# A 64-channel mix on four 64x64 quarters of TensorE's array, with the row sum issued ahead of it

## Chip, cores and metric

The kernel runs on one core of a Trainium2 chip. The metric is the device time of one execution in microseconds, the median over runs. Engines are called PE (TensorE: matmuls, with its weight loads shown apart as PEld), DVE (VectorE), ACT (ScalarE), POOL (GpSimd) and SP (SyncE, which here issues every DMA).

## What is computed

```
x        [64, 64, 1024] f32     itok     [64] int, 0..15
weights  [16, 64, 64]   f32     qweight  [1024, 768] int32 (6-bit values, 3 words -> 4 values)
scale, zero [1024, 1]           bias     [1024]

y   = einsum('bct,bcd->bdt', x, weights[itok])       # the "mix": a 64x64 matrix per batch entry
w   = (unpack6(qweight) - zero) * scale              # [1024, 1024]
out = x + einsum('bsk,nk->bsn', y, w) + bias
```

## The kernel before

**Tiles.** Two batch entries make a tile of 128 rows (entry 2t in partitions 0 to 63, entry 2t+1 in 64 to 127), so there are TILES = 32 tiles. The two 64x64 mixing matrices of a tile stand as blocks on the diagonal of `w_sb[:, slot, :]` (128x128, the other two blocks are zero; the DMAs of `load_w` fill only the diagonal). x, the mixing matrices and the results y have rings of RING = 4 slots.

**Mix.** `mix(j, i)` (L231) makes y transposed: for each of KT = 8 chunks of 128 positions, x's chunk is the stationary operand (128 rows of channels by 128 columns of positions) and the block-diagonal matrix is the moving one (128 columns). The result, 128 positions by 128 (entry, channel) columns, goes to `y_ps[:, j % 2, kt, :]`, a buffer of two PSUM banks per tile, used in turn by even and odd tiles. Both operands are f32. The trace shows two weight loads and two matmuls for each such call in the program, 16 pairs a tile. The semaphore `y_ps_ready` rises after chunk 3 and again after chunk 7.

**Row sum.** `sum_y` (L246) multiplies the same mixing matrices with a column of row sums of x (`xsum`, made by ACT at L336) into `ysum_ps`. It takes the zero point of the quantized weights out of the product later on (`residual`, L426).

**Splitting y.** ACT's `high` (L339) copies each half of y_ps to `y_hi` in the rounded type fp32r as soon as its semaphore rises; DVE's `low` (L417) subtracts it and writes the rest to `y_lo`.

**Linear layer.** `linear(j, i, h)` (L266) makes one 512-column half h of the output: 16 matmuls of 512 columns (8 chunks, y_hi and y_lo), from the unpacked integer weights `qT` in SBUF, into `o_ps[:, h]`. DVE multiplies it by the scale (`scale_out`, L434), adds the residual (`add_residual`, L445), and SP stores it. POOL adds x and bias into `resid` (L527).

**Order.** It is written out by hand for every engine. In the steady part `step(j, i)` of PE (L282) does the mix of the tile LEAD = 3 ahead, its row sum, and then the two halves of the linear layer of tile j. `mix` waits for x, for the mixing matrices, and for `y_lo` of the tile two before (its PSUM buffer); `linear(…, 0)` waits for `y_lo` of its own tile, `linear(…, h)` for the scaled output half of the tile before. Ahead of the loop a written-out start interleaves the first mixes with the unpacking and transposing of the quantized weights (`unpack_q` on DVE, `transpose_q` on PE, `place_q` on ACT). The last half of the last tile uses a y_ps bank as one of two 256-column output pieces.

Of the kernel before, what the change touches and what calls it, by code (L numbers as in the profile page):

```python
# [18 lines left out]
F32 = mybir.dt.float32  # L19
# [12 lines left out]
def adaln_ffn(nc: bass.Bass, x, cond, weights, qweight, scale, zero, bias, out):  # L32
# [19 lines left out]
    with ExitStack() as ctx:  # L52
# [6 lines left out]
        def sem(name):  # L59
# [20 lines left out]
        resid = sb("resid", [P, RING, N], F32)  # L80
        o_sb = sb("o_sb", [P, 2, N], F32)

        y_ps = psum("y_ps", [P, 2, KT, P], F32)
        o_ps = psum("o_ps", [P, H, NH], F32)
        ysum_ps = psum("ysum_ps", [P, 512], F32)
        qt_ps = psum("qt_ps", [P, KT, P], BF16)
# [3 lines left out]


        last_pieces = [(o_ps[:, 1, 0:NH // 2], NH, NH // 2),
                       (y_ps[:, 0, 0:KT // 2, :].rearrange("p t r -> p (t r)")[:, 0:NH // 2], NH + NH // 2, NH // 2)]


        ids_loaded = sem("ids_loaded")
# [132 lines left out]

        @block.tensor  # L230
        def _(pe):  # L231
            def mix(j, i):

                t = i * RING + j
                slot = j % RING
                x_arrived(pe, j, i)
                pe.wait_ge(w_loaded[slot], (i + j // RING + 1) * 32)
                if not isinstance(t, int) or t >= 2:
                    pe.wait_ge(y_lo_ready, (t - 1) * 2)
                for kt in range(KT):  # L240
                    last = nc.tensor.matmul(y_ps[:, j % 2, kt, :], x_sb[:, slot, kt * P:(kt + 1) * P],  # L241
                                            w_sb[:, slot, :], start=True, stop=True)
                    if kt % (KT // 2) == KT // 2 - 1:
                        last.then_inc(y_ps_ready, 1)

            def sum_y(j, i):  # L246

                t = i * RING + j
                slot = j % RING
                pe.wait_ge(w_loaded[slot], (i + j // RING + 1) * 32)  # L250
                pe.wait_ge(xsum_ready, t + 1)
                if not isinstance(t, int) or t >= 1:
                    pe.wait_ge(ysum_ready, t)
                nc.tensor.matmul(ysum_ps[:, slot:slot + 1], w_sb[:, slot, :], xsum[:, slot:slot + 1],  # L254
                                 start=True, stop=True).then_inc(ysum_ps_ready, 1)

            def transpose_q(n):
                pe.wait_ge(q_cast, n + 1)
                if n >= 2:
                    pe.wait_ge(qt_ready, n - 1)  # L260
                for kt in range(KT):
                    last = nc.tensor.transpose(qt_banks[n % 2][:, kt, :], q_bf[:, n % 4, kt * P:(kt + 1) * P],  # L262
                                               ident[:])
                last.then_inc(qt_ps_ready, 1)

            def linear(j, i, h):  # L266
                t = i * RING + j
                if h == 0:
                    pe.wait_ge(y_lo_ready, t * 2 + 2)
                if not isinstance(t, int) or t >= 1:  # L270
                    pe.wait_ge(scaled[h], t)
                products(o_ps[:, h, :], h * NH, NH, j % RING).then_inc(o_ps_ready[h], 1)

            def products(bank, col, width, slot):
                for kt in range(KT):
                    for part in (y_hi, y_lo):
                        last = nc.tensor.matmul(bank, part[:, slot, kt, :], qT[:, kt, col:col + width],  # L277
                                                start=(kt == 0 and part is y_hi),
                                                stop=(kt == KT - 1 and part is y_lo))
                return last  # L280

            def step(j, i, mixes=True):  # L282
                if mixes:
                    mix(j + LEAD, i)
                    sum_y(j + LEAD, i)
                for h in range(H):
                    linear(j, i, h)


            pe.wait_ge(warm_ready, 1)  # L290
            for _ in range(WARMUP):
                nc.tensor.matmul(ysum_ps[:], warm[:, 0:P], warm[:], start=True, stop=True)  # L292
            mix(0, 0)
            sum_y(0, 0)
            pe.wait_ge(ident_ready, 1)
            for n in range(NT // 2):
                transpose_q(n)
            mix(1, 0)
            pe.wait_ge(qt_ready, NT // 2)
            linear(0, 0, 0)  # L300
            sum_y(1, 0)
            mix(2, 0)
            sum_y(2, 0)
            transpose_q(4)
            transpose_q(5)
            linear(1, 0, 0)
            transpose_q(6)
            transpose_q(7)
            linear(2, 0, 0)
            mix(3, 0)  # L310
            sum_y(3, 0)
            pe.wait_ge(qt_ready, NT)
            for j in range(3):
                linear(j, 0, 1)
                mix(j + RING, 0)
                sum_y(j + RING, 0)
            for h in range(H):
                linear(3, 0, h)
            with pe.Fori(1, TRIPS - 1) as i:
                for j in range(RING):  # L320
                    step(j, i)
            for j in range(RING - 1):
                step(j, TRIPS - 1, mixes=j + LEAD < RING)
            linear(RING - 1, TRIPS - 1, 0)
            pe.wait_ge(scaled[1], TILES - 1)
            for bank, col, width in last_pieces:
                products(bank, col, width, RING - 1).then_inc(o_ps_ready[1], 1)


        @block.scalar  # L330
        def _(act):
            def sum_x(j, i):
                x_arrived(act, j, i)
                if not isinstance(i, int) or i * RING + j >= RING:
                    act.wait_ge(ysum_ps_ready, i * RING + j - RING + 1)
                nc.scalar.activation(junk[:], x_sb[:, j % RING, :], ACT.Copy,  # L336
                                     accum_out=xsum[:, j % RING:j % RING + 1]).then_inc(xsum_ready, 1)

            def high(j, i):  # L339
                t = i * RING + j  # L340
                for half in range(2):

                    act.wait_ge(y_ps_ready, t * 2 + half + 1)
                    chunks = slice(half * KT // 2, (half + 1) * KT // 2)
                    nc.scalar.activation(y_hi[:, j % RING, chunks, :], y_ps[:, j % 2, chunks, :],  # L345
                                         ACT.Copy).then_inc(y_hi_ready, 1)

            def copy_ysum(j, i):
                t = i * RING + j
                act.wait_ge(ysum_ps_ready, t + 1)  # L350
                if not isinstance(t, int) or t >= RING:
                    act.wait_ge(resid_ready, t - RING + 1)
                slot = j % RING
                nc.scalar.activation(ysum[:, slot:slot + 1], ysum_ps[:, slot:slot + 1],
                                     ACT.Copy).then_inc(ysum_ready, 1)

            def place_q(n):
                act.wait_ge(qt_ps_ready, n + 1)
                nc.scalar.activation(qT[:, :, n * P:(n + 1) * P], qt_banks[n % 2], ACT.Copy).then_inc(qt_ready, 1)

            sum_x(0, 0)
            high(0, 0)
            copy_ysum(0, 0)
            for n in range(NT // 2):
                place_q(n)
            high(1, 0)
            sum_x(1, 0)
            copy_ysum(1, 0)
            sum_x(2, 0)
            high(2, 0)  # L370
            copy_ysum(2, 0)
            place_q(4)
            place_q(5)
            sum_x(3, 0)
            place_q(6)
            place_q(7)
            high(3, 0)
            copy_ysum(3, 0)
            sum_x(4, 0)

            def step(j, i, highs=True, sums=True):
                if highs:
                    high(j + LEAD, i)
                    copy_ysum(j + LEAD, i)
                if sums:
                    sum_x(j + LEAD + 1, i)

            for j in range(1, RING):
                step(j, 0)
            with act.Fori(1, TRIPS - 1) as i:  # L390
                for j in range(RING):
                    step(j, i)
            step(0, TRIPS - 1, sums=False)
# [3 lines left out]
        def _(dve):  # L397
# [19 lines left out]
            def low(j, i):  # L417
                t = i * RING + j
                for half in range(2):
                    dve.wait_ge(y_hi_ready, t * 2 + half + 1)  # L420
                    chunks = slice(half * KT // 2, (half + 1) * KT // 2)
                    nc.vector.tensor_tensor(y_lo[:, j % RING, chunks, :], y_ps[:, j % 2, chunks, :],  # L422
                                            y_hi[:, j % RING, chunks, :].bitcast(F32),
                                            ALU.subtract).then_inc(y_lo_ready, 1)

            def residual(j, i):  # L426
# [131 lines left out]
```

## Time and profile before

| | us |
|---|---|
| median of 3 runs | 325.77 (323.64 to 326.3) |
| the profiled execution, its own time | 325.39 |
| its span, first to last instruction | 323.3 |
| mean granted TensorE clock (share of full) | 0.989 |

In the profile, PE's matmul records overlap, because one begins before the one ahead of it has left the array. The distance from start to start is what a matmul costs in a stream; the duration is how long it takes from its start to its last result. Weight loads (PEld) are records of their own beside the matmuls.

### The profile page before, as it was taken

To read this page: it belongs to the slowest core of one execution; us is meant where nothing else is said; L and a number is where in the kernel's file an instruction comes from. 1 tells how busy PE (TensorE), PEld (TensorE's weight loads), DVE (VectorE), ACT (ScalarE), POOL (GpSimd) and SP (SyncE) were. 2 spreads that over 40 slices of the span, in tenths; PEclk is the share of its full clock that TensorE was granted. 3 is DMA by queue.
4 is the path that set the end of the run, shared out by engine and by line. 5 is a ranking of instruction groups with operands and counts; after the bars stand their busy time and mean duration, and the time that the engine had idled before them with its cause. 6 is when DMAs were issued, how large, how long until landed. Compare 5 with 4: busy or idle time off the path is not lost.

```text
span 323.3 us, 5312 instructions
## 1 busy us (share of the span) xinstructions
PE 310.3 (96%) x1700; PEld 264.8 (82%) x1700; DVE 211.4 (65%) x261; ACT 82.6 (26%) x169; POOL 78.2 (24%) x39
## 2 busy tenths in 40 slices
PE   8892899999999999999999999999999999999995
PEld 3782788888888888888888888888888888888885
DVE  3589983776666667666666676666667766666553
ACT  3762153222221122222212222221122222210000
POOL 1009123222221222222112222221122222212000
PEclk9998699999999999999999999999999999999999
DMA  6992165532332333323333332233332311101122
GB/s 208 317 336 70 51 212 176 169 133 89 120 134 101 134 123 110 114 88 132 123 112 134 101 130 101 102 134 107 129 134 101 130 69 65 65 32 67 65 83 80
DMA packets 20684, 39.46 MB, mean 122 GB/s; under 512 B 6850, under 2 KB 7106, under 8 KB 20674
## 3 DMA queue, kind: packets, MB, share of 16 engines
q1 hardware_dynamic: 20674, 39.33, 35.1%
q8 instruction: 5, 0.08, 0.1%
q14 instruction: 5, 0.04, 0.0%
HBM read 22.54 MB, written 16.78 MB: 122 GB/s over the span
## 4 chain that ended last, share of the span: by engine, by line
PE 90%; DVE 5%; SPq 1%; DMA 1%; issue 1%; DVEq 0%
PE o_ps L277 72%; PE y_ps L241 17%; DMA q_raw<-in_L_ffn_qweight_dram 1%; DVE q_int L405 1%; DVE q_int L407 1%; DVE q_int L409 1%; PE ysum_ps L254 1%; DVE q_bf L414 1%; PE y_ps L277 1%; PE o_ps L262 1%; DVE y_lo L422 0%; SPq L145 0%; SPq L141 0%; SPq L136 0%; SPq L174 0%
## 5 line engine op out<-in xcount | busy, mean ns | idle before, releaser
L277 PE MATMUL o_ps<-qT,y_hi 128*128 128x512 f32 (+1 forms) x512 | 201.8, 395 | 0.0
L277 PE MATMUL o_ps<-qT,y_lo 128*128 128x512 f32 (+1 forms) x512 | 199.1, 390 | 0.0
L527 POOL TENSOR_TENSOR resid<-x_sb,bias_bc 128x1024 f32<-128x1024 f32 x32 | 77.0, 2411 | 213.8 <-DVE o_sb L450 192.2
L277 PEld LDWEIGHTS o_ps<-qT,y_lo 128*128 128x128 f32 x512 | 96.8, 189 | 19.1
L277 PEld LDWEIGHTS o_ps<-qT,y_hi 128*128 128x128 f32 x512 | 96.8, 189 | 18.9
L442 DVE TENSOR_TENSOR o_sb<-o_ps,scale_bc 128x512 f32<-128x512 f32 x63 | 43.6, 692 | 87.8 <-PE o_ps L277 87.8
L345 ACT ACTIVATE y_hi<-y_ps 128x512 fp32r<-128x512 f32 x64 | 38.3, 599 | 194.3 <-PE y_ps L241 194.3
L241 PEld LDWEIGHTS y_ps<-w_sb,x_sb 128*128 128x128 f32 x512 | 61.9, 191 | 2.4
L241 PE MATMUL y_ps<-w_sb,x_sb 128*128 128x128 f32 x512 | 62.4, 275 | 0.0
L431 DVE SCALAR_TENSOR_TENSOR resid<-zs_bc,ysum,resid 128x1024 f32<-128x1024 f32 x32 | 60.5, 1891 | 0.0
L422 DVE TENSOR_TENSOR y_lo<-y_ps,y_hi 128x512 fp32r<-128x512 f32 x64 | 44.0, 691 | 9.9 <-ACT y_hi L345 7.0
L450 DVE TENSOR_TENSOR o_sb<-o_sb,resid 128x512 f32<-128x512 f32 x63 | 43.6, 692 | 2.7 <-DVE resid L431 0.5
L336 ACT ACTIVATE junk<-x_sb 128x1024 bf16<-128x1024 f32 x32 | 33.9, 1059 | 3.3 <-DMA x_sb<-in_x_dram 3.3
L262 PE MATMUL o_ps<-ident,q_bf 128*128 128x128 bf16 x32 | 2.9, 242 | 7.8 <-DVE q_bf L414 7.8
L254 PEld LDWEIGHTS ysum_ps<-xsum,w_sb 128*128 128x128 f32 x64 | 9.8, 192 | 0.1
L405 DVE TENSOR_SCALAR q_int<-q_raw 128x256 int16<-128x256 int16 x8 | 5.5, 686 | 6.4 <-DMA q_raw<-in_L_ffn_qweight_dram 6.4
L254 PE MATMUL ysum_ps<-xsum,w_sb 128*128 128x1 f32 x64 | 9.0, 209 | 0.0
L262 PEld LDWEIGHTS o_ps<-ident,q_bf 128*128 128x128 bf16 x32 | 2.2, 109 | 8.1 <-DVE q_bf L414 8.1
L292 PE MATMUL ysum_ps<-warm 128*128 128x512 bf16 x20 | 7.1, 537 | 1.2 <-DVE warm L457 1.2
L292 PEld LDWEIGHTS ysum_ps<-warm 128*128 128x128 bf16 x20 | 2.5, 132 | 5.2 <-issue 3.5
L336 ACT ACTIVATION_READ_ACCUMULATOR junk<-x_sb 128x1 f32 x32 | 6.4, 200 | 0.0
L407 DVE TENSOR_SCALAR q_int<-q_raw 128x256 int16<-128x256 int16 x8 | 6.1, 763 | 0.0
(25 smaller groups left out, 42.7 us busy)
## 6 DMA issues: line engine op xcount, KB each, us to landing
x_sb<-in_x_dram SPq DMA_DIRECT2D x32, 512.0 KB, 3.3
out_dram<-o_sb SPq DMA_DIRECT2D x63, 256.0 KB, 2.0
q_raw<-in_L_ffn_qweight_dram SPq DMA_DIRECT2D x8, 384.0 KB, 4.7
w_sb<-in_L_cond_weights_dram SPq DMA_DIRECT2D x64, 16.0 KB, 2.0
scale_bc<-_L_ffn_weight_scale_dram SPq DMA_DIRECT2D x1, 512.0 KB, 5.1
zs_bc<-n_weight_zero_point_dram SPq DMA_DIRECT2D x1, 512.0 KB, 7.1
bias_bc<-in_L_ffn_bias_dram SPq DMA_DIRECT2D x1, 512.0 KB, 8.0
out_dram<-o_sb SPq DMA_DIRECT2D x2, 128.0 KB, 1.9
```

The lines of the kernel that those rows point to most:

```text
L241: last = nc.tensor.matmul(y_ps[:, j % 2, kt, :], x_sb[:, slot, kt * P:(kt + 1) * P], w_sb[:, slot, :], start=True, stop=True)
L254: nc.tensor.matmul(ysum_ps[:, slot:slot + 1], w_sb[:, slot, :], xsum[:, slot:slot + 1], start=True, stop=True).then_inc(ysum_ps_ready, 1)
L277: last = nc.tensor.matmul(bank, part[:, slot, kt, :], qT[:, kt, col:col + width], start=(kt == 0 and part is y_hi), stop=(kt == KT - 1 and ...
L292: nc.tensor.matmul(ysum_ps[:], warm[:, 0:P], warm[:], start=True, stop=True)
L336: nc.scalar.activation(junk[:], x_sb[:, j % RING, :], ACT.Copy, accum_out=xsum[:, j % RING:j % RING + 1]).then_inc(xsum_ready, 1)
L345: nc.scalar.activation(y_hi[:, j % RING, chunks, :], y_ps[:, j % 2, chunks, :], ACT.Copy).then_inc(y_hi_ready, 1)
L407: nc.vector.tensor_scalar(to[:, :, 1], words[:, :, 0, 0], QBITS, QMASK, ALU.logical_shift_right, ALU.bitwise_and).then_inc(q_part, 1)
L422: nc.vector.tensor_tensor(y_lo[:, j % RING, chunks, :], y_ps[:, j % 2, chunks, :], y_hi[:, j % RING, chunks, :].bitcast(F32), ALU.subtract ...
L431: nc.vector.scalar_tensor_tensor(resid[:, j % RING, :], zs_bc[:], ysum[:, j % RING:j % RING + 1], resid[:, j % RING, :], ALU.mult, ALU.add ...
L442: nc.vector.tensor_tensor(o_sb[:, j % 2, cols], o_ps[:, h, :], scale_bc[:, cols], ALU.mult).then_inc(scaled[h], 1)
L450: nc.vector.tensor_tensor(o_sb[:, j % 2, cols], o_sb[:, j % 2, cols], resid[:, j % RING, cols], ALU.add).then_inc(o_ready[h], 1)
L527: nc.gpsimd.tensor_tensor(resid[:, j % RING, :], x_sb[:, j % RING, :], bias_bc[:], ALU.add).then_inc(xbias_ready, 1)
```

## The change

The mix of a chunk is done as four calls in place of one. Row half `half` (64 partitions, one batch entry) and column half `part` (lower or upper 64 of the chunk's 128 positions) name a 64x64 quarter of the array; the stationary operand is 64 rows by 64 columns of x, the moving operand the 64x64 diagonal block of that entry. The zero blocks are no longer multiplied in the mix. y_ps is laid out with the entry ahead of the chunk, so that each row half writes a PSUM bank of its own; ACT's and DVE's two operations per tile now take one entry each (all 8 chunks, 64 of 128 columns of y_hi and y_lo) where they took four chunks each. Both increments of `y_ps_ready` are at the last chunk. The waits of the mix move to `wait_mix`, and in `step` the row sum goes between those waits and the mix.

```diff
--- before.py
+++ after.py
@@ -80,7 +80,7 @@
         resid = sb("resid", [P, RING, N], F32)
         o_sb = sb("o_sb", [P, 2, N], F32)
 
-        y_ps = psum("y_ps", [P, 2, KT, P], F32)
+        y_ps = psum("y_ps", [P, 2, 2, KT, S], F32)
         o_ps = psum("o_ps", [P, H, NH], F32)
         ysum_ps = psum("ysum_ps", [P, 512], F32)
         qt_ps = psum("qt_ps", [P, KT, P], BF16)
@@ -90,7 +90,7 @@
 
 
         last_pieces = [(o_ps[:, 1, 0:NH // 2], NH, NH // 2),
-                       (y_ps[:, 0, 0:KT // 2, :].rearrange("p t r -> p (t r)")[:, 0:NH // 2], NH + NH // 2, NH // 2)]
+                       (y_ps[:, 0, 0, :, :].rearrange("p t r -> p (t r)")[:, 0:NH // 2], NH + NH // 2, NH // 2)]
 
 
         ids_loaded = sem("ids_loaded")
@@ -229,19 +229,28 @@
 
         @block.tensor
         def _(pe):
-            def mix(j, i):
-
-                t = i * RING + j
-                slot = j % RING
+            def wait_mix(j, i):
+
+                t = i * RING + j
                 x_arrived(pe, j, i)
-                pe.wait_ge(w_loaded[slot], (i + j // RING + 1) * 32)
+                pe.wait_ge(w_loaded[j % RING], (i + j // RING + 1) * 32)
                 if not isinstance(t, int) or t >= 2:
                     pe.wait_ge(y_lo_ready, (t - 1) * 2)
+
+            def mix(j, i):
+
+                slot = j % RING
+                Q = P // 2
                 for kt in range(KT):
-                    last = nc.tensor.matmul(y_ps[:, j % 2, kt, :], x_sb[:, slot, kt * P:(kt + 1) * P],
-                                            w_sb[:, slot, :], start=True, stop=True)
-                    if kt % (KT // 2) == KT // 2 - 1:
-                        last.then_inc(y_ps_ready, 1)
+                    for part in range(2):
+                        for half in range(2):
+                            rows = slice(half * C, (half + 1) * C)
+                            k0 = kt * P + part * Q
+                            last = nc.tensor.matmul(y_ps[part * Q:(part + 1) * Q, j % 2, half, kt, :],
+                                                    x_sb[rows, slot, k0:k0 + Q], w_sb[rows, slot, rows],
+                                                    start=True, stop=True)
+                            if kt == KT - 1 and part == 1:
+                                last.then_inc(y_ps_ready, 1)
 
             def sum_y(j, i):
 
@@ -281,8 +290,9 @@
 
             def step(j, i, mixes=True):
                 if mixes:
+                    wait_mix(j + LEAD, i)
+                    sum_y(j + LEAD, i)
                     mix(j + LEAD, i)
-                    sum_y(j + LEAD, i)
                 for h in range(H):
                     linear(j, i, h)
 
@@ -290,15 +300,18 @@
             pe.wait_ge(warm_ready, 1)
             for _ in range(WARMUP):
                 nc.tensor.matmul(ysum_ps[:], warm[:, 0:P], warm[:], start=True, stop=True)
+            wait_mix(0, 0)
             mix(0, 0)
             sum_y(0, 0)
             pe.wait_ge(ident_ready, 1)
             for n in range(NT // 2):
                 transpose_q(n)
+            wait_mix(1, 0)
             mix(1, 0)
             pe.wait_ge(qt_ready, NT // 2)
             linear(0, 0, 0)
             sum_y(1, 0)
+            wait_mix(2, 0)
             mix(2, 0)
             sum_y(2, 0)
             transpose_q(4)
@@ -307,11 +320,13 @@
             transpose_q(6)
             transpose_q(7)
             linear(2, 0, 0)
+            wait_mix(3, 0)
             mix(3, 0)
             sum_y(3, 0)
             pe.wait_ge(qt_ready, NT)
             for j in range(3):
                 linear(j, 0, 1)
+                wait_mix(j + RING, 0)
                 mix(j + RING, 0)
                 sum_y(j + RING, 0)
             for h in range(H):
@@ -341,8 +356,8 @@
                 for half in range(2):
 
                     act.wait_ge(y_ps_ready, t * 2 + half + 1)
-                    chunks = slice(half * KT // 2, (half + 1) * KT // 2)
-                    nc.scalar.activation(y_hi[:, j % RING, chunks, :], y_ps[:, j % 2, chunks, :],
+                    cols = slice(half * S, (half + 1) * S)
+                    nc.scalar.activation(y_hi[:, j % RING, :, cols], y_ps[:, j % 2, half, :, :],
                                          ACT.Copy).then_inc(y_hi_ready, 1)
 
             def copy_ysum(j, i):
@@ -418,9 +433,9 @@
                 t = i * RING + j
                 for half in range(2):
                     dve.wait_ge(y_hi_ready, t * 2 + half + 1)
-                    chunks = slice(half * KT // 2, (half + 1) * KT // 2)
-                    nc.vector.tensor_tensor(y_lo[:, j % RING, chunks, :], y_ps[:, j % 2, chunks, :],
-                                            y_hi[:, j % RING, chunks, :].bitcast(F32),
+                    cols = slice(half * S, (half + 1) * S)
+                    nc.vector.tensor_tensor(y_lo[:, j % RING, :, cols], y_ps[:, j % 2, half, :, :],
+                                            y_hi[:, j % RING, :, cols].bitcast(F32),
                                             ALU.subtract).then_inc(y_lo_ready, 1)
 
             def residual(j, i):
```

## Rows read from the trace of the kernel before

**Rows 1.** Page, part 1: busy us (share of span) and instructions of each engine

```profile
PE 310.3 (96%) x1700; PEld 264.8 (82%) x1700; DVE 211.4 (65%) x261; ACT 82.6 (26%) x169; POOL 78.2 (24%) x39
```

**Rows 2.** Page, chain that ended last: shares by engine, then by line

```profile
PE 90%; DVE 5%; SPq 1%; DMA 1%; issue 1%; DVEq 0%
PE o_ps L277 72%; PE y_ps L241 17%; DMA q_raw<-in_L_ffn_qweight_dram 1%; DVE q_int L405 1%; DVE q_int L407 1%; DVE q_int L409 1%; PE ysum_ps L254 1%; DVE q_bf L414 1%; PE y_ps L277 1%; PE o_ps L262 1%; DVE y_lo L422 0%; SPq L145 0%; SPq L14
```

**Rows 3.** Page, groups: out<-in, shapes, count | busy us, mean ns | idle before

```profile
L277 PE MATMUL o_ps<-qT,y_hi 128*128 128x512 f32 (+1 forms) x512 | 201.8, 395 | 0.0
...
L241 PEld LDWEIGHTS y_ps<-w_sb,x_sb 128*128 128x128 f32 x512 | 61.9, 191 | 2.4
L241 PE MATMUL y_ps<-w_sb,x_sb 128*128 128x128 f32 x512 | 62.4, 275 | 0.0
...
L254 PE MATMUL ysum_ps<-xsum,w_sb 128*128 128x1 f32 x64 | 9.0, 209 | 0.0
```

**Rows 4.** Timeline of PE, one steady step: start us, us, what, count

```profile
158.34 0.39 PE L277 MATMUL o_ps<-qT,y_lo 128*128 128x512 f32 x1
158.57 1.95 PE L241 MATMUL y_ps<-w_sb,x_sb 128*128 128x128 f32 x16
160.35 0.28 PE L254 MATMUL ysum_ps<-xsum,w_sb 128*128 128x1 f32 x2
160.50 0.48 PE L277 MATMUL o_ps<-qT,y_hi 128*128 128x512 f32 x1
160.81 0.40 PE L277 MATMUL o_ps<-qT,y_lo 128*128 128x512 f32 x1
...
167.63 0.39 PE L277 MATMUL o_ps<-qT,y_lo 128*128 128x512 f32 x1
167.86 1.95 PE L241 MATMUL y_ps<-w_sb,x_sb 128*128 128x128 f32 x16
```

**Rows 5.** Timeline of PEld, and of PE's second L254 matmul, around the row sum

```profile
160.25 0.19 PEld L254 LDWEIGHTS ysum_ps<-xsum,w_sb 128*128 128x128 f32 x1
...
160.36 0.19 PEld L254 LDWEIGHTS ysum_ps<-xsum,w_sb 128*128 128x128 f32 x1
...
160.38 0.25 PE L254 MATMUL ysum_ps<-xsum,w_sb 128*128 128x1 f32 x1
...
160.47 0.19 PEld L277 LDWEIGHTS o_ps<-qT,y_hi 128*128 128x128 f32 x1
```

**Rows 6.** Timeline of PE, two tiles of transposes in a row

```profile
21.33 0.61 PE L262 MATMUL qt_ps<-ident,q_bf 128*128 128x128 bf16 x8
21.77 0.61 PE L262 MATMUL o_ps<-ident,q_bf 128*128 128x128 bf16 x8
22.19 0.47 PE L277 MATMUL o_ps<-qT,y_hi 128*128 128x512 f32 x1
```

**Rows 7.** Timeline of the start, PE and DVE; in brackets idle time and releaser

```profile
11.86 0.61 PE L262 MATMUL qt_ps<-ident,q_bf 128*128 128x128 bf16 x8 [0.76 <-DVE q_bf L414]
...
33.59 1.03 PE L262 MATMUL o_ps<-ident,q_bf 128*128 128x128 bf16 x8 [7.02 <-DVE q_bf L414]
...
19.45 0.69 DVE L442 TENSOR_TENSOR o_sb<-o_ps,scale_bc 128x512 f32<-128x512 f32 x1 [1.04 <-PE o_ps L277]
```

**Rows 8.** Timeline of ACT and DVE in the same steady step

```profile
159.66 0.60 ACT L345 ACTIVATE y_hi<-y_ps 128x512 fp32r<-128x512 f32 x1 [6.70 <-PE y_ps L241]
160.55 0.60 ACT L345 ACTIVATE y_hi<-y_ps 128x512 fp32r<-128x512 f32 x1 [0.29 <-PE y_ps L241]
...
160.29 0.69 DVE L422 TENSOR_TENSOR y_lo<-y_ps,y_hi 128x512 fp32r<-128x512 f32 x1
...
161.79 2.02 DVE L431 SCALAR_TENSOR_TENSOR resid<-zs_bc,ysum,resid 128x1024 f32<-128x1024 f32 x1
164.53 0.69 DVE L442 TENSOR_TENSOR o_sb<-o_ps,scale_bc 128x512 f32<-128x512 f32 x1 [0.72 <-PE o_ps L277]
```

## The prediction

> **What bounds the kernel now.** I read the page's busy shares first, then the chain that ended last, then the groups by cost, then the timeline of one steady step. PE is busy for 310.3 of 323.3 us [rows 1], and the chain is 90% PE: 72% linear layer (L277), 17% mix (L241), 1% row sum [rows 2]. The reader should see in the groups that PE's mix and linear matmuls have no idle time before them [rows 3]. So any time that PE gains or loses between 34 us and the end is gained or lost by the kernel, one for one.
>
> A steady step lasts 167.86 - 158.57 = 9.29 us [rows 4]. The linear layer's pace is (167.86 - 160.81) / 31 = 0.227 us a matmul, 7.28 us for 32. The rest, 2.01 us, is what the change works on: the mix, 160.35 - 158.57 = 1.78 us for 16 pairs of load and matmul, 0.111 us a pair; the row sum, 160.50 - 160.35 = 0.15 us; and a first linear matmul that holds the next one back to 0.31 us in place of 0.227, 0.08 us. That last piece exists because the first linear matmul cannot stream until its 128 columns of weights are in, while all others find them loaded.
>
> **Prices per pair.** A matmul record of the mix is 0.275 us long [rows 3] but they start 0.111 us apart [rows 4]: the stream costs 0.111, the way to the last result another 0.16. In the row sum the matmul has one column, and the loads still start 0.11 us apart (160.25, 160.36, 160.47) [rows 5]. So a load of 128 f32 columns costs 0.11 us by itself, as much as the 128 columns of matmul beside it; before, each hides the other. The matmuls of the row sum start at 160.35 and 160.38 with a load between them [rows 4, 5], so PE can hand out a load and a matmul 0.03 us apart, at least for once. Transposes, a bf16 load and matmul each, run at (21.77 - 21.33) / 8 = 0.055 us a pair [rows 6]; this bounds a sustained hand-out from above only.
>
> **What the change removes and adds on PE.** It removes 16 pairs of 128 columns a tile (8 calls, two passes each). It adds 32 calls, so 64 pairs, of 64 columns by 64 columns. I halve the 128-column prices: about 0.056 us to load, 0.056 us to stream. In total the tile now loads 64 x 64 = 4096 columns where it loaded 2048, and streams 64 x 0.056 = 3.58 us of matmuls where it streamed 1.78. Only quarters that work at the same time can pay this back. No row shows a matmul on part of the array, so the price is bounded from both sides:
> - Best: all four quarters run together. Each has 16 passes, 16 x 0.056 = 0.89 us.
> - In order, overlapping: the two passes of a call stand side by side in the program and use the same quarter, so the second waits 0.056 us for the first. Then the next quarter's first pass may start while the second pass streams. If that costs nothing, a call costs 0.056 and the mix 32 x 0.056 = 1.79 us. If it costs the 0.03 us between the row sum's two matmuls [rows 4, 5], a call costs 0.086 and the mix 32 x 0.086 = 2.75 us.
> - Loads one after another, each 0.056 us: 64 x 0.056 = 3.58 us.
> - No overlap of load and stream either: 64 x 0.112 = 7.2 us.
>
> I take 2.75 us. Of the four it rests on the nearest row (consecutive small matmuls with a load between), and it lies between the ends.
>
> What counts most is whether a matmul on a free quarter may pass one that waits for a busy quarter. The Trainium skill (TensorE: Matmul & The Clock Gate, The mechanism) says that matmuls start and end in program order, while loads may be pulled ahead when the row groups differ. The trace agrees as far as it goes, since all starts stand in program order [rows 4]. By the 4 ns between starts on different tiles that the same section of the Trainium skill gives, the mix would take 32 x 0.060 = 1.92 us.
>
> **The borders of the mix.** PE goes from the whole array to quarters and back once a step. No row shows such a switch. If it is free it costs 0. If the array has to empty first, each switch costs the 0.16 us that a result needs beyond its stream [rows 3, 4]. I take the full price, as loads for a differently divided array have nothing here that shows them overlapping, and keep 0 as the other end. The Trainium skill (TensorEngine Tiling (Array Packing), Key Properties) says that changing the tiling mode drains TensorE; this speaks against the change, and no row here can show it.
>
> The row sum now stands in front. Its first load hides behind the last linear matmul. Its second matmul starts 0.03 us on and is done 0.25 us later [rows 5], 0.28 after the first started; with a full drain the first quarter loads then, 0.056 us: 0.34 us until the mix streams. Without a drain it is the 0.11 of the second load plus 0.056, 0.17 us. Behind the mix come 0.16 us of drain and 0.11 us of load for the first linear matmul, 0.27 in place of 0.08; without a drain 0.08 as now. So the borders cost 0.61 us with drains and 0.25 without, where the row sum and the late matmul cost 0.23.
>
> **Sum of a step.** 0.34 + 2.75 + 0.27 = 3.36 us in place of 2.01: +1.35 us.
>
> **How many steps.** The mix of tile 0 lies ahead of a 0.76 us wait for unpacked weights; the mix of tile 2 ahead of the 7.02 us wait that DVE's unpacking ends [rows 7]. Both are covered. The mix of tile 1 lies on the path: the linear half behind it ends DVE's idle 1.04 us at 19.45 [rows 7], and DVE's remaining unpacking follows that. Tiles 3 to 31 have no gap. So 30 mixes count. 30 x 1.35 = 40.5 us on the profiled execution's 325.4 us (span 323.3 and 2.1 us around it), 366 us. Its time is 0.4 us under the median of the runs, which is less than their spread, so I leave it.
>
> **Costed at nothing.** ACT and DVE keep two operations a tile of the same element count; runs of 64 elements replace longer ones. Even at twice the price, 0.60 and 0.69 us more each, they add 1.2 us to ACT, which idled 6.70 us, and 1.4 us to DVE, which is 65% busy [rows 1, 8]. Both y_ps_ready increments now come at the mix's end, so ACT's first copy starts 0.89 us later than it did (159.66 against 160.55 [rows 8]) relative to that end. DVE's `low` and `residual` queue behind it, and `scale_out` of the first output half behind them. DVE waits 0.72 us ahead of that operation [rows 8], so it slips by 0.89 - 0.72, some 0.2 us; what waits for it is the next tile's linear half on PE, over 4 us later. y_lo itself is used three steps on. If this cover were gone, it would be 0.2 us a step, 6 us. `sum_y` in front needs x's row sum and the preceding ysum, both made in the step before: free. SP's reloads wait for y_ps_ready and ysum of a tile whose mix is long past.
>
> **Rivals.**
> 1. *Four quarters run together.* A pass on a free quarter does not wait for one that a busy quarter holds back. Step: 0.34 + 0.89 + 0.27 = 1.50 us, -0.51 x 30 = -15, 310 us; with free switches 0.17 + 0.89 + 0.08 = 1.14, -0.87 x 30 = -26, 299 us. It decides for "faster" once the mix takes under 1.40 us with drains (1.76 without), that is 22 ns (27 ns) a pair. For it speaks that half of today's products are zeros; against it, that a pair must be handed out faster than the 0.03 us the trace shows. The Trainium skill (TensorE: Matmul & The Clock Gate, Part 3) reports up to 10.6 times for sixteen 32x32 tiles, but with 512 columns each. Chance 0.24.
> 2. *Loads one at a time*, or a load never more than one matmul ahead, as all loads here start with the preceding matmul. Mix 3.58 us; step 4.19 or 3.83 (free switches); +65 or +55 us: 391 or 380 us. For it: the row sum shows loads as a serial resource of 0.11 us [rows 5]. Against it: those were loads to the same rows. Chance 0.27.
> 3. *The work doubles and the overlap halves it, switches free.* Mix 1.79, step 0.17 + 1.79 + 0.08 = 2.04 us, +0.03 x 30 = +1: 326 us. Chance 0.08.
> 4. *No overlap of load and stream.* 7.2 us a mix, step 7.4 to 7.8, some 490 us. The mix would double PE's work per step, and 0.111 us pairs show the hiding on the whole array. Chance 0.05.
>
> **How the numbers follow.** The forecast's mechanism, passes in order with some overlap, has 0.36. With the 0.03 us hand-over it gives 366 us with drains and 30 x (0.25 + 2.75 - 2.01) = +30, 355 us, without; with a free hand-over and drains 30 x (0.61 + 1.79 - 2.01) = +12, 337 us. Its own range is 337 to 366. The range over all reaches from rival 1 (299) to rival 2 (391); rival 4 and small spills stay out. About 1%, 3.3 us, is what a measurement of this kernel can tell from no change. Faster by over 1%: 0.24. Within 1%: 0.09. Slower: 0.67.
>
> **What would show it.** In the timeline of PE the step's length (9.29 now, 10.6 forecast) and the stretch from the first mix matmul to the first linear one: 0.9 to 1.2 us for rival 1, about 3 us for the forecast, 3.8 for rival 2. Starts within the mix that alternate 0.056 and 0.03 us show the in-order waiting; even ones of 0.056 the loads; even ones near 0.015 rival 1. A gap of 0.16 us or more at both borders shows the drain. The prediction is wrong if pairs are handed out faster than 0.03 us and quarters do not wait for each other.

## The result, and the profile after

The changed kernel takes 309.98 us (309.05 to 311.49 in 4 runs) against 325.32 us, a ratio of 0.954 (95% interval 0.948 to 0.960). The forecast was 366 us. The gain of 15 us lies in the range that was stated, but on the other side of no change, and it is almost to the microsecond what rival 1 gave with full drains (310 us).

The page of the changed kernel, first the shares, then the groups (out<-in, shapes, count | busy us, mean ns | idle before). L286 is the linear layer, L249 the mix, L263 the row sum:

```profile
PE 293.3 (95%) x3236; PEld 243.0 (79%) x3236; DVE 207.7 (67%) x261; ACT 79.1 (26%) x169; POOL 78.3 (25%) x39
...
PE o_ps L286 77%; PE y_ps L249 11%; DMA q_raw<-in_L_ffn_qweight_dram 1%; PE ysum_ps L263 1%; DVE q_int L422 1%; DVE q_int L420 1%; DVE q_int L424 1%; DVE q_bf L429 1%; PE y_ps L286 1%; PE o_ps L271 1%; DVE y_lo L437 0%; SPq L145 0%; SPq L141 0%; SPq L136 0%; SPq L174 0%
...
L249 PE MATMUL y_ps<-w_sb,x_sb 64*64 64x64 f32 x2048 | 37.8, 223 | 0.3 <-DMA w_sb<-in_L_cond_weights_dram 0.3
L249 PEld LDWEIGHTS y_ps<-w_sb,x_sb 64*64 64x64 f32 x2048 | 33.4, 136 | 2.6 <-issue 2.1
```

PE is still the bound (95% busy, [rows 1] had 96%). Its instructions went from 1700 to 3236 pairs, yet its mix fell from 62.4 us [rows 3] to 37.8, and from 17% [rows 2] to 11% of the chain.

One steady step on PE's timeline (start us, us, what, count), to be read against [rows 4]:

```profile
151.41 0.39 PE L286 MATMUL o_ps<-qT,y_lo 128*128 128x512 f32 x1
151.63 0.28 PE L263 MATMUL ysum_ps<-xsum,w_sb 128*128 128x1 f32 x2
151.84 1.16 PE L249 MATMUL y_ps<-w_sb,x_sb 64*64 64x64 f32 x64
152.93 0.50 PE L286 MATMUL o_ps<-qT,y_hi 128*128 128x512 f32 x1
153.27 0.40 PE L286 MATMUL o_ps<-qT,y_lo 128*128 128x512 f32 x1
...
160.36 0.28 PE L263 MATMUL ysum_ps<-xsum,w_sb 128*128 128x1 f32 x2
160.57 1.16 PE L249 MATMUL y_ps<-w_sb,x_sb 64*64 64x64 f32 x64
```

The step is 160.36 - 151.63 = 8.73 us in place of 9.29. The 64 mix matmuls span 1.16 us, and a settled one lasts 0.22, so they start within 0.94 us: 16 groups of four, 0.058 us a group, 0.015 us a matmul. Four narrow views of the same place show the group, where each row is the union of one more matmul, and what it ends behind:

```profile
151.84 0.27 PE L249 MATMUL y_ps<-w_sb,x_sb 64*64 64x64 f32 x1
...
151.84 0.27 PE L249 MATMUL y_ps<-w_sb,x_sb 64*64 64x64 f32 x2
...
151.84 0.28 PE L249 MATMUL y_ps<-w_sb,x_sb 64*64 64x64 f32 x3
...
151.84 0.29 PE L249 MATMUL y_ps<-w_sb,x_sb 64*64 64x64 f32 x4
```

Four matmuls of 0.27 us cover 0.29 us together: they start within 0.02 us and run side by side. There are two passes to each call in the program, 64 passes for 32 calls. Passes on the same quarter never start less than 0.058 us apart (eight calls in a row, below, show one quarter alone), so the four of a group stand on four different quarters. The second pass of quarter 0's call does not start next behind its first; the first passes of the other three quarters start before it.

**Where the 15 us are.** The end of the last matmul moved from 320.0 to 304.7 us. Tile 3's mix begins 0.73 us late (40.17 against 39.44) and brings 0.58, so that the linear half behind it is 0.15 us late (41.51 against 41.36). Tiles 4 to 6 brought 0.49 us each, the 25 tiles after them 0.56 each: -0.15 + 1.5 + 14.0 = 15.3 us.

The late start goes with a lower clock. From 14.1 to 17.4 us the granted clock was 0.50 in the changed kernel (its lower level, 1.2 GHz) and 1.00 in the kernel before; ahead of it PE had waited 2.25 and 0.74 us for unpacked weights, in the kernel before 0.76 and 0.74. The first two rows are that stretch, before and after: its bounds and length, busy us of PE, PEld, DVE, ACT and POOL, granted clock, DMA share, GB/s. The third is DVE's wait for the first linear half in the changed kernel, to be read against 19.45 in [rows 7].

```profile
14.10:17.40 3.30, 3.30 (x24) 2.96 (x23) 2.00 (x5) 2.94 (x5) 0.00 (x0) 1.00 1.04 407
14.10:17.40 3.30, 3.30 (x63) 2.79 (x54) 1.44 (x3) 2.61 (x4) 0.00 (x0) 0.50 0.95 320
20.46 0.69 DVE L457 TENSOR_TENSOR o_sb<-o_ps,scale_bc 128x512 f32<-128x512 f32 x1 [0.62 <-PE o_ps L286]
```

In that stretch the changed kernel took 1.72 us from tile 1's first mix matmul (13.77) to the linear layer's, where 1.09 is usual. How much of the 0.73 us this made is open: the kernel before with only the row sum moved (below) kept the clock at 1.00 there, and its tile 3's mix still began at 40.42.

### The profile page after: what moved, and what is told of

It reads as the page before. It is cut to its first block, busy times and chain, and to the rows that moved or that the text cites. A ratio compares the mean times of both kernels' runs of the same rounds, so it can differ in the third digit from the quotient of the medians.

```text
span 307.9 us, 8409 instructions
## 1 busy us (share of the span) xinstructions
PE 293.3 (95%) x3236; PEld 243.0 (79%) x3236; DVE 207.7 (67%) x261; ACT 79.1 (26%) x169; POOL 78.3 (25%) x39
## 4 chain that ended last, share of the span: by engine, by line
PE 90%; DVE 5%; SPq 1%; DMA 1%; issue 1%; DVEq 0%
PE o_ps L286 77%; PE y_ps L249 11%; DMA q_raw<-in_L_ffn_qweight_dram 1%; PE ysum_ps L263 1%; DVE q_int L422 1%; DVE q_int L420 1%; DVE q_int L424 1%; DVE q_bf L429 1%; PE y_ps L286 1%; PE o_ps L271 1%; DVE y_lo L437 0%; SPq L145 0%; SPq L141 0%; SPq L136 0%; SPq L174 0%
## 5 line engine op out<-in xcount | busy, mean ns | idle before, releaser
L286 PE MATMUL o_ps<-qT,y_hi 128*128 128x512 f32 (+1 forms) x512 | 203.7, 399 | 0.0
L286 PE MATMUL o_ps<-qT,y_lo 128*128 128x512 f32 (+1 forms) x512 | 200.1, 392 | 0.0
L286 PEld LDWEIGHTS o_ps<-qT,y_hi 128*128 128x128 f32 x512 | 97.0, 190 | 21.6
L286 PEld LDWEIGHTS o_ps<-qT,y_lo 128*128 128x128 f32 x512 | 97.1, 190 | 19.7
L360 ACT ACTIVATE y_hi<-y_ps 128x512 fp32r<-128x512 f32 x64 | 34.8, 596 | 181.4 <-PE y_ps L249 181.4
L437 DVE TENSOR_TENSOR y_lo<-y_ps,y_hi 128x512 fp32r<-128x512 f32 x64 | 41.2, 686 | 13.6 <-ACT y_hi L360 13.6
L249 PE MATMUL y_ps<-w_sb,x_sb 64*64 64x64 f32 x2048 | 37.8, 223 | 0.3 <-DMA w_sb<-in_L_cond_weights_dram 0.3
L249 PEld LDWEIGHTS y_ps<-w_sb,x_sb 64*64 64x64 f32 x2048 | 33.4, 136 | 2.6 <-issue 2.1
L263 PEld LDWEIGHTS ysum_ps<-xsum,w_sb 128*128 128x128 f32 x64 | 11.5, 188 | 2.7 <-issue 0.4
L263 PE MATMUL ysum_ps<-xsum,w_sb 128*128 128x1 f32 x64 | 9.4, 217 | 0.3 <-issue 0.3
L302 PE MATMUL ysum_ps<-warm 128*128 128x512 bf16 x20 | 5.8, 457 | 1.2 <-DVE warm L472 1.2
L369 ACT ACTIVATE ysum<-ysum_ps 128x1 f32<-128x1 f32 x32 | 5.7, 179 | 2.8 <-PE ysum_ps L263 2.8
```

Source lines behind the costliest of these rows:

```text
L249: last = nc.tensor.matmul(y_ps[part * Q:(part + 1) * Q, j % 2, half, kt, :], x_sb[rows, slot, k0:k0 + Q], w_sb[rows, slot, rows], start=Tr ...
L360: nc.scalar.activation(y_hi[:, j % RING, :, cols], y_ps[:, j % 2, half, :, :], ACT.Copy).then_inc(y_hi_ready, 1)
L437: nc.vector.tensor_tensor(y_lo[:, j % RING, :, cols], y_ps[:, j % 2, half, :, :], y_hi[:, j % RING, :, cols].bitcast(F32), ALU.subtract).t ...
```

## Experiments

Theory A: a quarter's passes wait only for their own quarter; others overtake them. Theory B: passes go in program order, and the four quarters overlap only because neighbouring calls name different quarters.

### Eight calls in a row on each quarter

```
-                for kt in range(KT):
-                    for part in range(2):
-                        for half in range(2):
+                for part, half, kt in [(p, h, k) for p in range(2) for h in range(2) for k in range(KT)]:
...
```

> Theory A (each quarter works for itself: a pass waits only for its own quarter, and passes for free quarters overtake it): the mix stays at 0.94 us, the step at 8.73 us, the time at 310 us. Theory B (passes reach the array in program order, and the four quarters run together only because four neighbouring calls name four different quarters): eight calls in a row on one quarter have nothing to overlap with, 64 passes of 0.058 us are 3.7 us of mix, 2.8 us more a step, 30 x 2.8 = 84 us more, about 394 us.

Measured: 375.95 us, ratio 1.153 (1.146 to 1.159). PE's timeline:

```profile
162.15 0.28 PE L261 MATMUL ysum_ps<-xsum,w_sb 128*128 128x1 f32 x2
162.35 3.40 PE L247 MATMUL y_ps<-w_sb,x_sb 64*64 64x64 f32 x64
165.69 0.50 PE L284 MATMUL o_ps<-qT,y_hi 128*128 128x512 f32 x1
```

The same 64 passes, the same operands, another order: 3.33 us from the first pass to the linear layer, where the changed kernel needs 1.09. A quarter's passes follow each other at 0.058 us and there is almost no overlap. Theory A, with a queue at each quarter deep enough for all of its passes, is ruled out. But it is not B either, which gave 3.7 us of passes: about 0.15 us of the 3.33 are the border behind the mix (1.09 - 0.94 in the changed kernel), which leaves 3.18.

### Two calls in a row, and four

```
+                for k2, part, half, kk in [(a, p, h, b) for a in range(KT // 2) for p in range(2)
+                                           for h in range(2) for b in range(2)]:
+                    kt = k2 * 2 + kk
...
```

> Two calls in a row on each quarter. Theory A: 310 us, mix 0.94 us. Theory B: the second call of each two waits for the first (two passes, 0.117 us) and holds back the next quarter; some 16 such waits, 1.9 us of mix, 30 x 0.93 = 28 us more, about 338 us. If the hardware looks ahead a little further than one call, the value lies between the two.

Measured: 313.77 us, ratio 0.962 (0.958 to 0.965).

```profile
162.55 1.30 PE L249 MATMUL y_ps<-w_sb,x_sb 64*64 64x64 f32 x64
...
163.78 0.50 PE L286 MATMUL o_ps<-qT,y_hi 128*128 128x512 f32 x1
...
162.55 0.31 PE L249 MATMUL y_ps<-w_sb,x_sb 64*64 64x64 f32 x4
```

1.23 us, close to A. The last row is a narrow view of the mix's beginning: the first four starts lie within 0.04 us (four matmuls of 0.27 cover 0.31 us), so quarters 1 to 3 begin although quarter 0 has a whole second call outstanding.

The same with four in a row (`KT // 4`, `range(4)`):

> Four calls in a row on each quarter. With one call in a row the mix takes 1.09 us from its first to the linear layer's first matmul, with two 1.23, with eight 3.33. Theory A' (passes for a free quarter overtake waiting ones, but only from a limited number of calls behind): four in a row lies clearly above two, near 2.4 to 3.0 us, 340 to 360 us. Rival (each quarter has a deep queue and eight in a row are slow for some other reason): close to two in a row, 1.3 to 1.5 us, 315 us.

Measured: 354.68 us, ratio 1.087 (1.082 to 1.092).

```profile
164.59 2.69 PE L249 MATMUL y_ps<-w_sb,x_sb 64*64 64x64 f32 x64
167.20 0.50 PE L286 MATMUL o_ps<-qT,y_hi 128*128 128x512 f32 x1
```

2.61 us. The rival (a deep queue) is out.

### One entry after the other

```
+                for half, kt, part in [(h, k, p) for h in range(2) for k in range(KT) for p in range(2)]:
...
```

> All 16 calls of entry 0 (two quarters in turn), then all of entry 1, so that only two quarters have work near each other. Limited look-ahead: two groups of 16 passes a quarter, 32 x 0.058 = 1.87 us, less a little at the seam, 0.85 us a step more than with four quarters in turn, about 335 us. Rival (deep queues for each quarter): 310 us.

Measured: 330.25 us, ratio 1.012 (1.008 to 1.017); 1.84 us from the mix's first matmul to the linear layer's. That is 0.75 us more than with four quarters in turn, where 0.85 was expected; the gain at the one seam was taken too small. Two quarters in turn make half the overlap of four, and the kernel is about 1% slower than with no quarters at all.

**One number fits these orders.** Take off the border's 0.15 us and compare with what no overlap (64 x 0.058 = 3.74 us) or two by two (32 x 0.058 = 1.87) would be, counting the places where the program moves on to another quarter or pair of quarters:

| calls in a row | seams | passes took, us | without overlap at seams, us | saved a seam, us |
|---|---|---|---|---|
| 8 | 3 | 3.18 | 3.74 | 0.19 |
| 4 | 7 | 2.46 | 3.74 | 0.18 |
| 2 | 15 | 1.08 | 3.74 | 0.18 |
| entry outer | 1 | 1.69 | 1.87 | 0.18 |
| 1 (the change) | 31 | 0.94 | 3.74 | at the floor, 16 x 0.058 |

Each change of quarter overlaps 0.18 us, three passes of 0.058, until the four quarters are full. So theory A', the limited look-ahead, holds: work for a free quarter goes ahead once no more than three passes are left at a busy one; more than that block everything behind.

The narrow views show the three left, and that the limit is one for each quarter. In the first pair of rows (eight calls in a row; views from 162.354 us to 163.105 and to 163.110) 13 passes have started, and then a fourteenth within 0.01 us. It is too close to be on the same quarter, so the next quarter begins with three of quarter 0's 16 passes left. In the second pair (one entry after the other; views from 162.45 us to 163.208 and to 163.212) the twenty-seventh pass starts within about 0.01 us of the last on either busy quarter, so on a third one, with 6 of the first entry's 32 passes left, three at each of two quarters:

```profile
162.35 0.97 PE L247 MATMUL y_ps<-w_sb,x_sb 64*64 64x64 f32 x13
162.35 1.02 PE L247 MATMUL y_ps<-w_sb,x_sb 64*64 64x64 f32 x14
...
162.45 0.97 PE L247 MATMUL y_ps<-w_sb,x_sb 64*64 64x64 f32 x26
162.45 1.03 PE L247 MATMUL y_ps<-w_sb,x_sb 64*64 64x64 f32 x27
```

With two calls in a row the fourth quarter starts with nine earlier passes still to come, three at each of three quarters. A common window over all passes would have one size; these need 3, 6 and 9. Three waiting passes at each quarter fit all orders tried.

### One dimension divided alone

Row halves, in the changed kernel (64 rows by 128 columns stationary, two calls a chunk):

```
+                    for half in range(2):
+                        rows = slice(half * C, (half + 1) * C)
+                        last = nc.tensor.matmul(y_ps[:, j % 2, half, kt, :],
+                                                x_sb[rows, slot, kt * P:(kt + 1) * P], w_sb[rows, slot, rows], ...
```

> Row halves alone: 64 rows by all 128 columns stationary, two calls a chunk. If the two halves load at the same time, each does 16 passes bound by a 128-column load of 0.111 us: mix 1.78 us, 30 x 0.84 = 25 us more than with quarters, about 335 us. If their loads go one after the other, 32 x 0.111 = 3.6 us, about 388 us. If the array drains at the borders also in this division, the row sum and the first linear matmul look as with quarters.

Measured: 334.77 us, ratio 1.026 (1.022 to 1.031).

```profile
164.37 0.28 PE L261 MATMUL ysum_ps<-xsum,w_sb 128*128 128x1 f32 x2
164.57 2.00 PE L247 MATMUL y_ps<-w_sb,x_sb 64*128 64x64 f32 x32
166.50 0.50 PE L284 MATMUL o_ps<-qT,y_hi 128*128 128x512 f32 x1
```

Column halves, in the kernel before with the row sum in front (128 rows by 64 columns stationary, all 128 columns moving):

```
+                    for part in range(2):
+                        k0 = kt * P + part * Q
+                        last = nc.tensor.matmul(y_ps[part * Q:(part + 1) * Q, j % 2, kt, :],
+                                                x_sb[:, slot, k0:k0 + Q], w_sb[:, slot, :], ...
```

> Column halves alone: all 128 rows by 64 columns stationary, the block-diagonal matrix of 128 columns moving, two calls a chunk, row sum in front of the mix, y_ps as in the kernel before. If the two column halves stream at the same time, each has 16 passes bound by a 0.111 us stream: mix 1.78 us, about 335 us. If there is one stream for both, 32 x 0.111 = 3.6 us, about 388 us.

Measured: 333.14 us, ratio 1.021 (1.016 to 1.026).

```profile
162.84 1.97 PE L247 MATMUL y_ps<-w_sb,x_sb 128*64 128x128 f32 x32
164.74 0.50 PE L284 MATMUL o_ps<-qT,y_hi 128*128 128x512 f32 x1
```

Both came out as the first branch said; from first mix matmul to linear layer they take 1.93 and 1.90 us, with the same 0.15 of border in it. Row halves halve the stream and leave the 128-column load, which sets the pace: 32 pairs in about the 1.8 us of 16 before, so two loads into different rows run at the same time. Column halves halve the load and leave the 128-column stream, and two streams into different columns run at the same time. Either alone leaves the mix at its old 1.8 us and adds the borders. Only when both halve does the mix shrink.

### The row sum's place

In the kernel before, nothing but `sum_y` moved in front of `mix` in `step`, behind the mix's waits:

> The kernel before, with nothing but the row sum moved in front of the mix. Theory A (the move is neutral by itself and the quarters are the whole gain): the second load of the row sum still costs 0.11 us and the mix's first matmul now waits 0.08 us for its load where the linear layer's first did; ratio to the kernel before 1.00 (325 us). Rival: the move itself brings a part of the gain by hiding a load, 0.1 us a step, 3 us, ratio 0.99.

Measured: 326.71 us, ratio 1.002 (0.998 to 1.006). The step is 9.31 us in place of 9.29. By itself the move brings nothing.

Quarters, with the row sum behind:

```
-                    wait_mix(j + LEAD, i)
+                    mix(j + LEAD, i)
                     sum_y(j + LEAD, i)
-                    mix(j + LEAD, i)
...
+                linear(j, i, 0)
+                if not isinstance(i, int):
+                    wait_mix(j + LEAD + 1, i)
+                linear(j, i, 1)
```

> Quarters, with the row sum behind the mix as it was (the mix's own waits stand a half linear layer earlier, where they are long met). Adding up prices read from the changed kernel (0.09 us of emptying at each border, 0.11 us for each uncovered 128-column load): three such loads behind the mix in place of one ahead and one behind, +0.11 us a step, 30 x 0.11 = 3 us, 313 us. Rival: the place of the row sum makes no difference, 310 us.

Measured: 312.3 us, ratio 0.955 (0.951 to 0.959).

```profile
153.22 1.16 PE L249 MATMUL y_ps<-w_sb,x_sb 64*64 64x64 f32 x64
...
162.02 1.16 PE L249 MATMUL y_ps<-w_sb,x_sb 64*64 64x64 f32 x64
```

The step is 8.79 us, 0.07 more than the change's 8.73, where 0.11 was expected. So 0.49 of the change's 0.56 us a step come without the row sum's new place. Over 28 steps the 0.07 are 2 us, less than the intervals of the two ratios can part.

The row sum on the two diagonal quarters, in front of the mix, with all waits ahead of the linear layer's second half:

```
+                for half in range(2):
+                    rows = slice(half * C, (half + 1) * C)
+                    last = nc.tensor.matmul(ysum_ps[rows, slot:slot + 1], w_sb[rows, slot, rows],
+                                            xsum[rows, slot:slot + 1], start=True, stop=True)
...
```

> The row sum too is done on quarters: two calls on the two diagonal quarters, directly ahead of the mix. Theory A: the border moves ahead of the row sum, two more passes of 0.058 us on two of the quarters replace a 0.11 us load, so the step is the same within 0.05 us, 309 to 311 us. Rival: passes on the other two quarters start while the row sum's are under way, the row sum costs nothing, 0.1 us a step, 307 us.

Measured: 308.51 us, ratio 0.944 (0.941 to 0.947). The step is 8.67 us, 0.05 less than the change's. On the timeline the mix's first two matmuls start between the row sum's:

```profile
160.87 0.22 PE L274 MATMUL ysum_ps<-xsum,w_sb 64*64 64x1 f32 x2
160.88 0.27 PE L249 MATMUL y_ps<-w_sb,x_sb 64*64 64x64 f32 x2
160.94 0.20 PE L274 MATMUL ysum_ps<-xsum,w_sb 64*64 64x1 f32 x2
```

The two quarters that the row sum leaves free start on the mix at once. A part of the row sum is hidden, about half of the 0.1 us of the rival; the step alone would also fit theory A (the same within 0.05 us), but the starts between the row sum's are the rival's. The earlier waits changed along with it.

### What the borders cost

The row sum in the middle of the mix, two more switches a step, with the waits where they stand in the run with the row sum behind:

```
+                    mix(j + LEAD, i, range(KT // 2))
                     sum_y(j + LEAD, i)
+                    mix(j + LEAD, i, range(KT // 2, KT))
```

> Quarters, with the row sum in the middle of the mix, after chunk 3: two more switches of the array's division in every step than with the row sum at the edge. Theory A (a switch costs 0.09 us of emptying and lays the next load bare): beside the row sum behind the mix (step 8.79 us) it adds 0.09 + 0.09 + 0.06 us, some 0.2 to 0.25 us a step, to 9.0 us, 30 x 0.22 = 7 us more, 319 us. Rival (a switch is free and only loads cost): the step stays at 8.8 us, 312 us.

Measured: 318.36 us, ratio 0.976 (0.973 to 0.979).

```profile
164.19 0.69 PE L249 MATMUL y_ps<-w_sb,x_sb 64*64 64x64 f32 x32
164.81 0.38 PE L263 MATMUL ysum_ps<-xsum,w_sb 128*128 128x1 f32 x2
165.12 0.69 PE L249 MATMUL y_ps<-w_sb,x_sb 64*64 64x64 f32 x32
165.75 0.50 PE L286 MATMUL o_ps<-qT,y_hi 128*128 128x512 f32 x1
```

The step is 164.19 - 155.14 = 9.05 us, 0.25 more than with the row sum behind the mix: 0.13 us a switch, bare quarter load included. A switch costs, and costs less than the 0.16 us of drain plus load (0.22 or 0.27 us) that the prediction took.

Then the other way, half as many switches. The mixes of tiles t+2 and t+3 stand side by side in every even step, the row sum of t+3 comes a step later, and ACT, DVE and SP are reordered to match:

```
+                if mixes and j % 2 == 0:
+                    wait_mix(j + 2, i)
+                    wait_mix(j + 3, i)
+                    sum_y(j + 2, i)
+                    mix(j + 2, i)
+                    mix(j + 3, i)
+                elif mixes:
+                    sum_y(j + 2, i)
```

> The mixes of two tiles stand side by side in every second step, so that the array is switched to quarters and back half as often (128 passes in one go). Theory A (each border costs 0.09 us of emptying and an uncovered load): per two steps it saves two times 0.09, a 0.06 us quarter load and up to a 0.11 us whole load, 0.24 to 0.35 us, times 14: 3.5 to 5 us, 305 to 307 us. Rival: the borders are not what costs, or ACT and DVE, which now get two tiles at once, hold PE back: 310 us or more.

Measured: 306.66 us (305.06 to 307.3), ratio 0.937 (0.933 to 0.942).

```profile
159.32 0.28 PE L263 MATMUL ysum_ps<-xsum,w_sb 128*128 128x1 f32 x2
...
166.82 0.28 PE L263 MATMUL ysum_ps<-xsum,w_sb 128*128 128x1 f32 x2
167.03 2.10 PE L249 MATMUL y_ps<-w_sb,x_sb 64*64 64x64 f32 x128
...
176.48 0.28 PE L263 MATMUL ysum_ps<-xsum,w_sb 128*128 128x1 f32 x2
```

Two steps take 176.48 - 159.32 = 17.16 us, 0.30 less than twice 8.73, where 0.24 to 0.35 was expected. PE has no wait in this part. It beats both kernels.

### The change once more

> The changed kernel itself, on the chip of these runs: 310 us, ratio to the kernel before 0.954.

Measured: 309.99 us (309.94 to 310.63), ratio 0.951 (0.948 to 0.953). Its interval doesn't touch that of the paired mixes (0.933 to 0.942), each against the kernel before on its own chip. Its steady step is 8.73 us again and its last matmul ends at 304.8, though its start went otherwise: the granted clock was 0.50 from 11.8 to 15 and from 39.1 to 49.2 us, and PE's long wait for DVE came later (7.29 us, up to 44.66).

## Why the prediction was wrong, point by point

- **What bounds the kernel: right.** In the profiled execution PE has no gap from 34 us on. Time on PE went one for one into the result.
- **The mix, 2.75 us: wrong, and nearly the whole error.** It measures 0.94 us; that is 1.81 of the 1.95 us by which the step's sum of 3.36 was too long. The step that failed stands in "In order, overlapping": the second pass of a call waits 0.056 us for the first and only then "the next quarter's first pass may start". The groups of four show that a call's second pass holds nobody back, and two and four calls in a row show how far that goes: three waiting passes at a quarter. The sentence that starts stand in program order [rows 4] was weak evidence. With the whole array every pass needs the same quarters, so these rows could not tell the two cases apart, and they should not have carried 0.36 against 0.24.
- **The hand-out, 0.03 us: wrong.** The 0.03 us between the row sum's two matmuls [rows 4, 5] has a wait in it: a matmul may start 0.03 us behind the start of its own load, and that load had to wait its turn. Here four pairs are handed out in 0.02 us, and the sustained pace is 0.015 us a pair. It was used as the nearest row, but against the break-even of 0.022 us a pair a row that holds a wait is only an upper bound, as the transposes' was.
- **Halved prices, 0.056 us to load and to stream: right.** A quarter's passes come at 0.058 us; loads run together in different rows, streams in different columns. Rival 2's serial loads (3.58 us) are out.
- **Borders and row sum, 0.61 us with drains: right kind, somewhat large.** Linear pace 31 x 0.229 = 7.09 us; 8.73 - 7.09 - 0.23 = 1.41 us for row sum, mix and borders; less 0.94, the borders and the row sum cost 0.47 us, where the kernel before paid 0.23. The rule of the Trainium skill (TensorEngine Tiling (Array Packing), Key Properties), that a change of the tiling mode drains TensorE, agrees so far as a switch costs 0.13 us by the row sum in the middle. But the next matmul's record does not wait for the last result of the old division: the first linear matmul starts 0.15 us behind the mix's last start, and that matmul's record lasts 0.22. The two sides together, 0.47 us, lie between the prediction's 0.61 and its 0.25 without a drain.
- **30 steps: close.** The 29 mixes from tile 3 on count, with 0.49 to 0.58 us each, 16.1 us together. The mix of tile 1 does lie on the path, as predicted: DVE waited 0.62 us for the linear half behind it, until 20.46. It gave nothing in the profiled execution, where the granted clock was 0.50; the start as a whole cost 0.73 us, which the sum did not have.
- **ACT and DVE at nothing: right.** DVE's wait ahead of `scale_out` of the first half shrank from 0.72 us [rows 8] to 0.15, and was not used up.
- **The rule cited for the forecast.** The Trainium skill (TensorE: Matmul & The Clock Gate, The mechanism) says matmuls start and end in program order. For calls on different quarters the trace disagrees: with one call in a row, all four quarters' first passes start before any second pass, and with two in a row they start before quarter 0's second call. Its 4 ns between starts on different tiles is near the 0.02 us for three gaps here (7 ns each, with two passes to a call).

Rival 1's sum (0.34 + 0.89 + 0.27 = 1.50 us) came out at 1.41, plus 0.04 us of slower linear matmuls over the step. Its mechanism is the one that the runs show; that its 310 us was met within a microsecond is in part luck. Its mix was 0.05 us short and its borders 0.14 long, and the 16.1 us that the mixes gave, less the 0.73 us of the late start, come to its 15.3.

Left open: how much of the late start is the lower clock; whether the two row halves need a PSUM bank each (writing one bank from both wasn't tried), and what part of 2 to 3 us in the row-sum variants comes from the earlier place of the waits, which wasn't tried by itself.

## What to carry to other kernels

When an operand is block-diagonal or small in both dimensions, divide the array in both: halving only rows left the load as the bound and halving only columns the stream, and both were slower than before. Issue calls so that neighbours name different quarters, with at most two in a row on one (four passes: one at work, three waiting); the same 32 calls took 0.94 us or 3.2 us by their order alone. Put work of one division side by side, since each switch cost about 0.13 us, and before taking a row as a price, ask whether it could have looked otherwise if the rival were true.

## What the runs showed of the hardware that was not expected

- Pairs of weight load and matmul start 0.007 us apart on four different quarters, and keep up 0.015 us a pair over 64 pairs (128 in the paired mixes: 2.10 us less a last matmul of 0.22, 0.0147 us each).
- The overlap at a change of quarter is three passes of 0.058 us, in all four orders tried. A quarter can have three passes waiting without holding back calls for the others: the next quarter started with 3, 6 and 9 earlier passes still to come, three at each busy quarter.
- The two passes of an f32 call need not stand together: passes of other quarters' calls come between them.
